# Giving GpSimd the fourth token tile of each batch when the expert results are mixed

## The chip, the cores and the metric

The kernel runs on one core of one Trainium2 chip. The metric is the device time of one execution in microseconds (us). Five engines share the work: TensorE (PE, matrix products into PSUM), VectorE (DVE), ScalarE (ACT), GpSimd (POOL) and SyncE (SP), which here only issues DMAs. They run side by side and meet at semaphores.

## The reference

The program is two transformer layers over 8 batches of 512 tokens with 128 features, in float32. Each layer is attention and then a mixture of experts, with a residual sum around both. The expert part of layer 0 picks 2 of 16 experts for each token, that of layer 1 picks 2 of 8:

```python
x = x + _L0_attn_ref(_layernorm(x), ...)
x = x + _L0_ffn_ref(_layernorm(x), ...)     # 16 experts, top 2
x = x + _L1_attn_ref(_layernorm(x), ...)
x = x + _L1_ffn_ref(_layernorm(x), ...)     # 8 experts, top 2
...
# layer 1's mixture, the same in its last step as layer 0's
topk_values, topk_indices = jax.lax.top_k(router_logits, TOP_K)
topk_weights = jax.nn.softmax(topk_values, axis=-1)
...
mixed_output = jnp.sum(topk_expert_outputs * topk_weights[..., None], axis=2)
```

What matters here is the last step of each mixture: for every token, two result rows of 128 numbers, each times the token's weight for that expert, added to the token's row of `x`.

## The kernel before

`X` holds all 4096 tokens in SBUF as 32 tiles of 128 tokens (128 partitions) by 128 features. A batch is `T` = 4 tiles, and there are `B` = 8 batches. The program is four stages, one after the other, each in a block of its own with a barrier of all engines at its end, after which GpSimd clears the stage's semaphores one by one (line 65): attention of layer 0, `experts` for layer 0 (tag L0), attention of layer 1, `experts` for layer 1 (tag L1).

`experts` routes the tokens, scatters them to DRAM sorted by expert (`x_d`), runs the two matrix products of each expert on tiles of 128 rows, and lets GpSimd scatter every finished tile to its tokens' places in DRAM (`y_d`, indirect DMAs of line 2010). When the last scatter has landed, the stage ends in a mix, and only this mix is touched by the change:

- SyncE's `load(i)` (line 1944) brings the results of batch `i` into one of `MB` = 4 slots of `got`: two DMAs of 256 KB, one for each of the `CH` = 2 chosen experts. The first four batches are loaded at once; the load of batch `i + 4` waits until batch `i` is mixed, since it takes the same slot. All DMAs of the mix are issued from SyncE's queue, in the order of its program.
- VectorE (line 2225) does, for each batch, 4 tiles of the first expert and then 4 tiles of the second, one instruction for a tile, `X = got * gate + X` with both tensors in SBUF. Between the two halves it waits for `mixed1`, since the second half reads what the first has written.
- In the mix of layer 1, SyncE's `write(i)` (line 1949) sends batch `i` of `X` to the output, 256 KB, as soon as it is mixed. In SyncE's queue stand `write(0)`, `load(4)`, `write(1)`, `load(5)` and so on. The mix of layer 0 has no writes.

GpSimd, ScalarE and TensorE have nothing to do in a mix. GpSimd's last work before it is the last scatter.

Of the kernel before, what the change touches and what calls it, by code (L numbers as in the profile page):

```python
# [10 lines left out]
ALU = mybir.AluOpType  # L11
# [5 lines left out]
B, S = 8, 512  # L17
T = S // P
# [55 lines left out]
def build(nc, ins, out, phases="ABCD"):  # L74
    ctx = ExitStack()
    with ctx:
# [29 lines left out]
        if "B" in phases:  # L106
            experts(nc, ins, common, "L0", E0, out)
        if "C" in phases:
            layer1_attention(nc, ins, common)
        if "D" in phases:  # L110
            experts(nc, ins, common, "L1", E1, out)
# [1689 lines left out]
def experts(nc, ins, c, tag, E, out):  # L1801
# [8 lines left out]
    with ExitStack() as ctx:  # L1810
        def sb(name, shape, dt=F32):
            return ctx.enter_context(nc.sbuf_tensor(f"{tag}_{name}", shape, dt))
# [3 lines left out]
        def flag(name):  # L1816

            flags.append(ctx.enter_context(nc.semaphore(f"{tag}_{name}")))
            return flags[-1]

        def after(eng, signal, n):

            if n > 0:
                eng.wait_ge(signal, n)
# [3 lines left out]
        CH = 2  # L1828
# [3 lines left out]
        XB, RB, GB, WB, YB, MB = len(c[f"{tag}_put"]), 2, 6, 4, len(c[f"{tag}_scattered"]), 4  # L1832
        assert NT <= P

        X, ident = c["X"], c["ident"]
# [18 lines left out]
        gate = sb("gate", [P, CH, NG])  # L1854
# [26 lines left out]
        got = sb("got", [P, MB, CH, T, D])  # L1881
# [16 lines left out]
        hidden, acted, y, y_set = flag("hidden"), flag("acted"), flag("y"), flag("y_set")  # L1898
        y_loaded = [flag(f"y_loaded{n}") for n in range(MB)]
        mixed1, mixed2, written = flag("mixed1"), flag("mixed2"), flag("written")  # L1900
        LOADS = 16 * (2 * 4 + 2)
        MADE = 13

# [8 lines left out]
        @block.sync  # L1912
        def _(sp):
            sp.dma_start(wr[:, :], ins[f"{tag}_wr"]).then_inc(wr_loaded, 16)
            if first:
                sp.dma_start(br[:, :], ins["L0_br"].partition_broadcast(P)).then_inc(br_loaded, 16)
            sp.wait_ge(made, 2)
            sp.dma_start(x_d.rearrange("(e r) c -> r e c", e=E)[0:P], empty).then_inc(cleared, 16)
            sp.dma_start(W1[:, :, F + FC:], ins[f"{tag}_b2"].partition_broadcast(P)).then_inc(loads, 16)
            sp.dma_start(W1[:, :, F:F + FC], ins[f"{tag}_b1"]).then_inc(loads, 16)  # L1920
            for n in range(4):
                es = slice(n * E // 4, (n + 1) * E // 4)
                sp.dma_start(W1[:, es, 0:F], ins[f"{tag}_w1"][:, es, :]).then_inc(loads, 16)
                sp.dma_start(W2[:, es, :, :], ins[f"{tag}_w2"][:, es, :, :]).then_inc(loads, 16)

            sp.wait_ge(listing, 1)
            for n in range(XB):
                sp.wait_ge(put[n], 16 * CH * T * len(range(n, B, XB)))
            for n in range(NT):
                at = sp.value_load(slots[0:1, 1, n:n + 1], min_val=0, max_val=E * CAP - P)  # L1930
                if n >= GB:
                    sp.wait_ge(g_turned, n - GB + 1)
                    sp.wait_ge(di_set, n - GB + 1)
                sp.dma_start(xg[:, n % GB, :], x_d[bass.ds(at, P), :]).then_inc(gathered[n % GB], 16)

            for n in range(YB):
                sp.wait_ge(scattered[n], 16 * len(range(n, NT, YB)))
            results = y_d[0:CH * TOK].rearrange("(k n p) d -> p k n d", k=CH, p=P)
            rows = out.rearrange("(n p) d -> p n d", p=P)

            def load(i):
                after(sp, mixed2, T * (i - MB + 1))
                for k in range(CH):
                    sp.dma_start(got[:, i % MB, k, :, :], results[:, k, i * T:(i + 1) * T, :]
                                 ).then_inc(y_loaded[i % MB], 16)

            def write(i):
                sp.wait_ge(mixed2, T * (i + 1))
                sp.dma_start(rows[:, i * T:(i + 1) * T, :], X[:, i * T:(i + 1) * T, :]).then_inc(written, 16)

            for i in range(MB):
                load(i)
            for i in range(B):
                if not first:
                    write(i)
                if i + MB < B:
                    load(i + MB)
            if not first:
                sp.wait_ge(written, 16 * B)

        @block.gpsimd
        def _(pool):
            exact = dict(allow_small_or_imprecise_dtypes=True)
            pool.memset(empty[:, :, 0:D], 0.0).then_inc(made, 1)
            pool.iota(empty[:, :, D:ROW].bitcast(I32), pattern=[[P, E], [0, 1]], base=CH * TOK + NT * P, channel_multiplier=1
                      ).then_inc(made, 1)
            pool.iota(spare[:, :], pattern=[[P, NT]], base=CH * TOK, channel_multiplier=1, **exact).then_inc(made, 1)
            pool.iota(desc[:, :, :], pattern=[[0, T], [-1, E]], base=E, channel_multiplier=0, **exact).then_inc(made, 1)
            pool.iota(dest[:, :, :], pattern=[[P, NG], [TOK, CH]], base=0, channel_multiplier=1).then_inc(made, 1)
            pool.iota(cursor[:, 0, :], pattern=[[CAP, E]], base=0, channel_multiplier=0, **exact).then_inc(made, 1)  # L1970
            pool.iota(column[:, 0:1], pattern=[[0, 1]], base=0, channel_multiplier=1, **exact).then_inc(made, 1)
            pool.iota(column[:, 1:2], pattern=[[0, 1]], base=0, channel_multiplier=P, **exact).then_inc(made, 1)
            pool.memset(tiles[:, :, 0:E], 0.0).then_inc(made, 1)
            pool.memset(ones[:, :], 1.0).then_inc(made, 1)
            pool.memset(ones32[:, :], 1.0).then_inc(made, 1)
            pool.memset(tri[:, :], 1.0).then_inc(made, 1)
            pool.wait_ge(made, 12)

            pool.affine_select(out=tri[:, :], in_=tri[:, :], compare_op=ALU.is_gt, fill=0.0,
                               base=0, pattern=[[1, P]], channel_multiplier=-1).then_inc(made, 1)  # L1980

            def root(i):
                pool.wait_ge(mean, T * (i + 1))
                after(pool, scaled, T * (i - RB + 1))
                pool.tensor_tensor(ve[:, i % RB, :], mv[:, i % RB, :, 1], c["eps"][:, :], ALU.add).then_inc(eps_added, 1)
                pool.wait_ge(eps_added, i + 1)
                pool.tensor_tensor(rstd[:, i % RB, :], ve[:, i % RB, :], c["half"][:, :], ALU.pow).then_inc(rooted, 1)  # L1987

            def put_rows(i):
                if i == 0:  # L1990
                    pool.wait_ge(cleared, 16)
                pool.wait_ge(scaled, T * (i + 1))
                pool.wait_ge(tagged, i + 1)
                pool.wait_ge(placed, i + 1)
                for k in range(CH):
                    for t in range(T):
                        pool.indirect_dma_start(x_d, bass.IndirectOffsetOnAxis(place_i[:, i % XB, k, t:t + 1], 0),  # L1997
                                                XN[:, i % XB, t, k, :], None).then_inc(put[i % XB], 16)

            root(0)  # L2000
            root(1)
            for i in range(B):
                if i + 2 < B:
                    root(i + 2)
                put_rows(i)

            for n in range(NT):
                pool.wait_ge(di_set, n + 1)
                pool.wait_ge(y_set, n + 1)
                pool.indirect_dma_start(y_d, bass.IndirectOffsetOnAxis(di[:, n % YB:n % YB + 1], 0),  # L2010
                                        ys[:, n % YB, :], None).then_inc(scattered[n % YB], 16)

        @block.scalar
        def _(act):
# [29 lines left out]
        def _(dve):  # L2044
# [131 lines left out]
            dve.wait_ge(listing, 2)  # L2176
            dve.wait_ge(loads, LOADS)

# [39 lines left out]
            for i in range(B):  # L2218
                dve.wait_ge(y_loaded[i % MB], 16 * CH * (i // MB + 1))
                for k, mixed in enumerate((mixed1, mixed2)):  # L2220
                    if k:
                        dve.wait_ge(mixed1, T * (i + 1))
                    for t in range(T):
                        n = i * T + t
                        dve.scalar_tensor_tensor(X[:, n, :], got[:, i % MB, k, t, :], gate[:, k, n:n + 1], X[:, n, :],  # L2225
                                                 ALU.mult, ALU.add).then_inc(mixed, 1)
            dve.wait_ge(mixed2, B * T)

        @block.tensor
        def _(pe):  # L2230
# [45 lines left out]
            pe.wait_ge(listing, 2)  # L2276
            pe.wait_ge(loads, LOADS)

# [118 lines left out]
```

## Time and profile before

| | us |
|---|---|
| median of 3 runs | 2020.45 |
| lowest and highest of them | 2016.98, 2028.79 |
| the profiled execution's own time | 2031.6 |
| its span in the trace | 2029.3 |

The time of a run is that of an execution without the profiler; the profile is one further execution. Its span is from the first to the last instruction that the trace shows, and 2.3 us of its own time lie around the span. An instruction's duration is from its start to its end; VectorE starts the next one before the last has ended, so that the distance between starts is shorter than a duration. "Idle before" a group is time in which its engine waited, and the name behind the arrow is what ended the wait. The two mixes lie near 956 to 980 us and near 2000 to 2026 us of the span.

### The profile page before, as it was taken

To read this page: it belongs to the slowest core of one execution; us is meant where nothing else is said; L and a number is where in the kernel's file an instruction comes from. 1 tells how busy PE (TensorE), PEld (TensorE's weight loads), DVE (VectorE), ACT (ScalarE), POOL (GpSimd) and SP (SyncE) were. 2 spreads that over 40 slices of the span, in tenths; PEclk is the share of its full clock that TensorE was granted. 3 is DMA by queue.
4 is the path that set the end of the run, shared out by engine and by line. 5 is a ranking of instruction groups with operands and counts; after the bars stand their busy time and mean duration, and the time that the engine had idled before them with its cause. 6 is when DMAs were issued, how large, how long until landed. Compare 5 with 4: busy or idle time off the path is not lost. (4 is left out here: it accounts for less than half of the span.)

```text
span 2029.3 us, 39821 instructions
## 1 busy us (share of the span) xinstructions
PE 1520.3 (75%) x11726; PEld 979.1 (48%) x11726; DVE 1270.2 (63%) x3477; ACT 892.7 (44%) x1807; POOL 681.3 (34%) x773
## 2 busy tenths in 40 slices
PE   2699999999997423998136898788888979333993
PEld 0223333333333222998024566566665656323993
DVE  2578777777773364554415686877767867353555
ACT  0166666665665001654222555545544434102652
POOL 2202221121100374555153334333433310374552
PEclk9999999999999555999557999999999989756997
DMA  3211111111100531222242434444344441411225
GB/s 93 55 52 52 52 37 40 50 35 51 52 25 1 125 136 45 73 72 79 75 121 88 114 109 127 120 131 121 107 125 116 125 113 47 115 48 50 72 70 148
DMA packets 121565, 165.68 MB, mean 82 GB/s; under 512 B 21458, under 2 KB 94962, under 8 KB 120786
## 3 DMA queue, kind: packets, MB, share of 16 engines
q1 hardware_dynamic: 112530, 145.69, 25.1%
q0 software_dynamic: 8896, 18.30, 2.7%
q8 instruction: 67, 1.10, 0.2%
q14 instruction: 72, 0.59, 0.1%
HBM read 116.04 MB, written 47.60 MB: 81 GB/s over the span
## 5 line engine op out<-in xcount | busy, mean ns | idle before, releaser
L648 DVE TENSOR_REDUCE a_M<-a_F 128x1 f32<-128x512 f32 x512 | 325.7, 682 | 73.7 <-PE a_F L790 72.3
L557 ACT ACTIVATE a_PT<-a_ST 128x512 f32<-128x512 f32 x512 | 276.8, 594 | 137.0 <-PE a_ST L830 134.8
L1392 ACT ACTIVATE c_PT<-c_ST 128x1024 f32<-128x1024 f32 x160 | 163.4, 1021 | 205.7 <-PE c_ST L1702 157.3
L2040 ACT ACTIVATE L_hT<-L_P,L_W1s 128x128 f32<-128x128 f32 x600 | 171.9, 369 | 147.8 <-issue 91.1
L2010 POOL DMA_INDIRECT L_yd<-L_ys,L_di x150 | 163.2, 1088 | 151.6 <-issue 101.9
L830 PE MATMUL a_ST<-a_QS,a_KS 74*128 74x512 bf16 x512 | 173.6, 396 | 21.6 <-ACT a_PT L557 10.0
L790 PE MATMUL a_F<-a_KS,a_QS 72*128 72x512 bf16 x512 | 166.1, 402 | 8.8 <-DVE a_M L648 8.5
L1701 PE MATMUL c_ST<-ident,c_SD 128*128 128x128 f32 x512 | 146.9, 287 | 26.9 <-issue 17.3
L2289 PE MATMUL L_P<-L_xT,L_W1s 128*128 128x128 f32 x1200 | 161.8, 279 | 0.4 <-issue 0.4
L2298 PE MATMUL L_P<-L_W,L_hT 128*128 x1200 | 160.3, 277 | 0.1
L2289 PEld LDWEIGHTS L_P<-L_xT,L_W1s 128*128 128x128 f32 x1200 | 149.5, 196 | 0.7 <-issue 0.7
L2298 PEld LDWEIGHTS L_P<-L_W,L_hT 128*128 128x128 f32 x1200 | 147.3, 193 | 0.6 <-issue 0.4
L809 PE MATMUL a_PV<-a_PT,a_V 128*32 128x512 f32 x1024 | 142.1, 629 | 1.0 <-ACT a_PT L557 1.0
L1997 POOL DMA_INDIRECT L_xd<-L_XN,L_place_i x128 | 124.4, 972 | 53.2 <-issue 37.1
L830 PEld LDWEIGHTS a_ST<-a_QS,a_KS 74*128 74x128 bf16 x512 | 44.0, 98 | 175.0 <-ACT a_PT L557 120.8
L2183 DVE TENSOR_SCALAR L_W1s<-L_W 128x644 f32 x150 | 74.5, 497 | 80.7 <-issue 68.8
L1500 DVE TENSOR_TENSOR c_inc<-c_INC,c_table 128x512 f32<-128x512 f32 x128 | 87.6, 685 | 59.2 <-PE c_INC L1669 58.7
L1702 PE MATMUL c_ST<-c_less,c_pick 128*128 128x128 bf16 x512 | 114.8, 224 | 0.0
L1708 PE MATMUL c_ST<-c_QS,c_KS 126*128 126x384 bf16 (+2 forms) x384 | 108.3, 282 | 0.0
L1707 PE MATMUL c_ST<-c_less,c_pick 128*128 128x384 bf16 (+2 forms) x384 | 107.7, 281 | 0.0
L1513 DVE TENSOR_TENSOR c_SD<-c_DIAG,c_inc 128x512 f32<-128x512 f32 x128 | 87.3, 682 | 25.9 <-PE c_ST L1708 25.9
L1675 PE MATMUL c_DIAG<-c_KS,c_QS 72*128 72x128 bf16 x512 | 76.8, 227 | 34.1 <-DVE c_SD L1513 34.1
(282 smaller groups left out, 3107.2 us busy)
## 6 DMA issues: line engine op xcount, KB each, us to landing
c_QS<-c_q SPq DMA_DIRECT2D x32, 504.0 KB
c_QS<-c_rd SPq DMA_DIRECT2D x32, 378.0 KB
L_xg<-L_xd SPq DMA_DIRECT2D x150, 64.5 KB
a_QS<-a_q SPq DMA_DIRECT2D x32, 288.0 KB
a_KS<-a_k SPq DMA_DIRECT2D x96, 96.0 KB
c_KS<-c_k SPq DMA_DIRECT2D x96, 96.0 KB
L_W<-in_L_w SPq DMA_DIRECT2D x8, 1024.0 KB
L_got<-L_yd SPq DMA_DIRECT2D x32, 256.0 KB, 4.6
```

Source lines behind the costliest of these rows:

```text
L557: act.activation(PT[:, j, kk, :], ST[:, kk, :], ACT.Exp).then_inc(sem(exped), 1)
L648: dve.tensor_reduce(M[:, t, h:h + 1], FB[n % BANKS][:, :], AX_X, ALU.max).then_inc(sem(maxed), 1)
L790: pe.matmul(FB[n % BANKS][:, :], QS[0:STACK, h, t * P:(t + 1) * P], KS[0:STACK, h, :], start=True, stop=True).then_inc(sem(filled), 1)
L809: last = pe.matmul(PV[32 * j:32 * j + 32, :], V[:, kt, QUAD * g + j, :], PT[:, QUAD * (kt // 2) + j, kt % 2, :], start=(kt == 0), stop=(kt ...
L830: pe.matmul(ST[:, kk, :], KS[0:KR0, h, kt * P:(kt + 1) * P], QS[0:KR0, h, :], start=True, stop=True).then_inc(sem(scored), 1)
L1392: act.activation(PT[:, j, :, :], ST[:, :, :], ACT.Exp).then_inc(sem(exped), 1)
L1701: pe.matmul(out, SD[:, g % 2, j, t, :], ident[:, :], start=True, stop=False, is_transpose=True)
L1997: pool.indirect_dma_start(x_d, bass.IndirectOffsetOnAxis(place_i[:, i % XB, k, t:t + 1], 0), XN[:, i % XB, t, k, :], None).then_inc(put[i ...
L2010: pool.indirect_dma_start(y_d, bass.IndirectOffsetOnAxis(di[:, n % YB:n % YB + 1], 0), ys[:, n % YB, :], None).then_inc(scattered[n % YB], 16)
L2040: act.activation(hT[:, n % 2, f, :], PS[2 + 2 * (n % 2) + f // 2][:, (f % 2) * P:(f % 2 + 1) * P], func, bias=W1s[:, n % WB, F + f:F + f + ...
L2289: last = pe.matmul(PS[2 + 2 * (n % 2) + f // 2][:, (f % 2) * P:(f % 2 + 1) * P], W1s[:, n % WB, f * P:(f + 1) * P], xT[:, n % 3, :], start ...
L2298: last = pe.matmul(PS[6 + n % 2][:, 0:D], hT[:, n % 2, f, :], W2[:, bass.ds(e, 1), f, :].rearrange("p a d -> p (a d)"), start=(f == 0), st ...
```

## The change

Of the four tiles of a batch VectorE now mixes three (`OWN` = 3), with the same instructions. GpSimd takes the fourth, and as it is written here it needs two instructions for each expert where VectorE needs one: it multiplies the result tile by the weight in place (`weighed`), and adds it to `X` (`added_up`). The second add waits for the first, and both wait for their product. `load` and `write` now wait for both engines.

```diff
+        weighed, added_up = flag("weighed"), flag("added_up")
+        OWN = T - 1
...
             def load(i):
-                after(sp, mixed2, T * (i - MB + 1))
+                after(sp, mixed2, OWN * (i - MB + 1))
+                after(sp, added_up, CH * (i - MB + 1))
...
             def write(i):
-                sp.wait_ge(mixed2, T * (i + 1))
+                sp.wait_ge(mixed2, OWN * (i + 1))
+                sp.wait_ge(added_up, CH * (i + 1))
...
+            for i in range(B):
+                n = i * T + OWN
+                pool.wait_ge(y_loaded[i % MB], 16 * CH * (i // MB + 1))
+                for k in range(CH):
+                    pool.tensor_scalar(got[:, i % MB, k, OWN, :], got[:, i % MB, k, OWN, :], gate[:, k, n:n + 1], None,
+                                       ALU.mult).then_inc(weighed, 1)
+                for k in range(CH):
+                    pool.wait_ge(weighed, CH * i + k + 1)
+                    after(pool, added_up, CH * i + k)
+                    pool.tensor_tensor(X[:, n, :], X[:, n, :], got[:, i % MB, k, OWN, :], ALU.add).then_inc(added_up, 1)
+            pool.wait_ge(added_up, CH * B)
...
                     if k:
-                        dve.wait_ge(mixed1, T * (i + 1))
-                    for t in range(T):
+                        dve.wait_ge(mixed1, OWN * (i + 1))
+                    for t in range(OWN):
...
-            dve.wait_ge(mixed2, B * T)
+            dve.wait_ge(mixed2, B * OWN)
```

VectorE's instructions at the start of layer 0's mix, before:

```order
L2225 SCALAR_TENSOR_TENSOR X<-L_got,L_gate,X 128x128 [waits L0_y_loaded0]
L2225 SCALAR_TENSOR_TENSOR X<-L_got,L_gate,X 128x128 x3
L2225 SCALAR_TENSOR_TENSOR X<-L_got,L_gate,X 128x128 [waits L0_mixed1]
L2225 SCALAR_TENSOR_TENSOR X<-L_got,L_gate,X 128x128 x3
L2225 SCALAR_TENSOR_TENSOR X<-L_got,L_gate,X 128x128 [waits L0_y_loaded1]
```

The same place now:

```order
L2241 SCALAR_TENSOR_TENSOR X<-L_got,L_gate,X 128x128 [waits L0_y_loaded0]
L2241 SCALAR_TENSOR_TENSOR X<-L_got,L_gate,X 128x128 x2
L2241 SCALAR_TENSOR_TENSOR X<-L_got,L_gate,X 128x128 [waits L0_mixed1]
L2241 SCALAR_TENSOR_TENSOR X<-L_got,L_gate,X 128x128 x2
L2241 SCALAR_TENSOR_TENSOR X<-L_got,L_gate,X 128x128 [waits L0_y_loaded1]
```

Each batch has lost two of its eight instructions there, and the waits stand where they stood. GpSimd's instructions at the end of layer 0's expert stage, which before went from the 79 scatters straight to the block's end, are now:

```order
L2014 DMA L_yd<-L_ys,L_di 20352x128 [waits L0_y_set,L0_di_set] x79
L2021 TENSOR_SCALAR L_got<-L_got,L_gate 128x128 [waits L0_y_loaded0]
L2021 TENSOR_SCALAR L_got<-L_got,L_gate 128x128
L2026 TENSOR_TENSOR X<-X,L_got 128x128 [waits L0_weighed]
L2026 TENSOR_TENSOR X<-X,L_got 128x128 [waits L0_added_up,L0_weighed]
L2021 TENSOR_SCALAR L_got<-L_got,L_gate 128x128 [waits L0_y_loaded1]
```

So 32 instructions have been added to GpSimd in each mix, four for a batch, behind its last scatter.

## Rows read from the trace of the kernel before

**Rows 1.** The page's head: the span, and the whole run's busy time of each engine

```profile
span 2029.3 us, 39821 instructions
...
PE 1520.3 (75%) x11726; PEld 979.1 (48%) x11726; DVE 1270.2 (63%) x3477; ACT 892.7 (44%) x1807; POOL 681.3 (34%) x773
```

**Rows 2.** The groups of instructions in layer 0's mix (956.7:984), then in layer 1's (2000:2030)

```profile
L2225 DVE SCALAR_TENSOR_TENSOR X<-L_got,L_gate,X 128x128 f32<-128x128 f32 x64 | 17.7, 348 | 7.7 <-DMA L_got<-L_yd 7.4
...
L2225 DVE SCALAR_TENSOR_TENSOR X<-L_got,L_gate,X 128x128 f32<-128x128 f32 x64 | 17.7, 347 | 7.4 <-DMA L_got<-L_yd 7.1
```

**Rows 3.** The chain that ended last, from 2000 us: start, length, what

```profile
2002.95 4.71 DMA L_got<-L_yd
...
2008.86 2.20 DVE X L2225 x8
...
2011.08 2.20 DVE X L2225 x8
...
2022.21 1.14 DVE X L2225 x4
```

**Rows 4.** The timeline of SyncE's queue, layer 1's mix

```profile
2007.50 0.38 SPq L1949 DMA_DIRECT2D out_x<-X  x1
...
2007.92 1.34 SPq L1944 DMA_DIRECT2D L_got<-L_yd  x2
```

**Rows 5.** DMA issues from 2000 us: KB each, median us to landing

```profile
L_got<-L_yd SPq DMA_DIRECT2D x16, 256.0 KB, 4.5
```

**Rows 6.** One stretch of layer 1's mix: busy times, granted PE clock, DMA share, GB/s

```profile
2005.00:2019.50 14.50, 0.00 (x0) 0.00 (x0) 13.92 (x51) 0.00 (x0) 0.00 (x0) 0.50 1.12 321
```

**Rows 7.** GpSimd's groups by shape, whole run

```profile
L431 POOL TENSOR_TENSOR a_rot<-a_rot,a_part 128x512 f32<-128x512 f32 x16 | 18.5, 1158 | 35.2 <-ACT a_part L514 35.2
...
L1250 POOL TENSOR_TENSOR c_power<-c_power,c_length 128x128 f32<-128x128 f32 x24 | 10.9, 456 | 1.9
...
L1250 POOL TENSOR_TENSOR c_power<-c_guess 128x128 f32<-128x128 f32 x24 | 9.6, 401 | 55.6 <-DVE c_guess L1457 54.4
...
L1205 POOL TENSOR_SCALAR_AFFINE_SELECT c_table<-c_table 128x2048 f32<-128x2048 f32 x1 | 2.0, 2007 | 7.3 <-ACT c_table L1290 7.3
...
L129 POOL TENSOR_SCALAR_AFFINE_SELECT ident<-ident 128x128 f32<-128x128 f32 x1 | 0.3, 287 | 0.2 <-issue 0.2
```

**Rows 8.** GpSimd's timeline where each instruction waits for the one before

```profile
1038.48 0.46 POOL L1250 TENSOR_TENSOR c_power<-c_power,c_length 128x128 f32<-128x128 f32 x1
1039.01 0.45 POOL L1250 TENSOR_TENSOR c_power<-c_power,c_three_halves 128x128 f32<-128x128 f32 x1
```

**Rows 9.** VectorE's groups by shape, 1040:1050

```profile
L1477 DVE TENSOR_TENSOR c_LP<-c_line,c_DQ 128x384 f32<-128x384 f32 x1 | 0.6, 550 | 0.0
...
L1474 DVE TENSOR_TENSOR c_LP<-c_line,c_DQ 128x96 f32<-128x96 f32 x1 | 0.3, 251 | 0.0
```

**Rows 10.** Timelines near 1215 and 1236 us; last, L1521's min/median/max ns

```profile
1215.23 1.15 POOL L1263 TENSOR_TENSOR c_part<-c_rem,c_part 96x512 bf16<-96x512 f32 x1 [1.50 <-ACT c_part L1342]
...
1216.20 0.21 DVE L1521 TENSOR_TENSOR c_MD<-c_MD,c_M 128x12 f32<-128x12 f32 x1
...
1236.23 0.17 DVE L1521 TENSOR_TENSOR c_MD<-c_MD,c_M 128x12 f32<-128x12 f32 x1
...
L1521 DVE TENSOR_TENSOR c_MD<-c_MD,c_M x32: 160/170/216, 1095.5 to 1720.3; 128x12 f32<-128x12 f32 x32
```

**Rows 11.** Near 654 us: GpSimd's timeline, then VectorE's L169, min/median/max ns

```profile
653.94 1.26 POOL L447 TENSOR_TENSOR a_XC<-a_XA,a_b 128x512 f32<-128x512 f32 x1
...
L169 DVE TENSOR_SCALAR a_ZN<-a_XA,a_tmv,a_trstd x4: 335/336/1207, 654.1 to 655.7; 128x128 f32<-128x128 f32 x4
```

**Rows 12.** Timeline near 722 us, GpSimd and VectorE

```profile
722.69 1.04 POOL L1987 TENSOR_TENSOR L_rstd<-L_ve,half 128x4 f32<-128x4 f32 x1
722.79 0.23 DVE L2079 TENSOR_TENSOR L_eq<-L_work,L_gate 128x64 f32<-128x64 f32 x1
723.05 0.23 DVE L2080 TENSOR_TENSOR L_eq<-L_eq,L_desc 128x64 f32<-128x64 f32 x1
```

**Rows 13.** The clears of semaphores, whole run, min/median/max ns

```profile
L65 POOLq EVENT_SEMAPHORE_RANGE_CLEAR  x219: 37/38/47, 678.1 to 2028.9; - x110
```

## The prediction

> **What bounds the kernel now.** I began with the page's head, to have the span of the profiled execution (2029.3 us) and to see that over the whole run GpSimd is a third busy [rows 1]. That average says nothing of a mix, so I went to the groups of each mix by itself. In both, VectorE runs 64 instructions, 17.7 us busy, and waits 7.7 and 7.4 us, nearly all of it for the first loads [rows 2]. Nothing else computes there. The chain of waits shows what counts: from the last load's landing on, it consists of VectorE alone, eight instructions after eight, to the last one at 2022.21 + 1.14 = 2023.35 us [rows 3]. A batch of eight takes 2011.08 - 2008.86 = 2.22 us, 0.278 us for each, and a mix 8 x 2.22 = 17.8 us [rows 3]. So both mixes lie on the path in full, and what shortens a batch's mix there shortens the kernel. The two mixes are 35.6 us of 2029.3, 1.8%: the whole lever of this change.
>
> The engine that paces the mix is not alone near its limit. The 16 DMA engines are shown full in layer 1's mix, at 321 GB/s [rows 6]. And the slots make a ring: batch 0 was done at 2007.50, when SyncE issued its write; the two loads that reuse its slot were issued from 2007.92 to 2009.26, and a load takes 4.5 us from issue to landing [rows 4, 5]. The second was issued at about 2008.5 and so landed near 2013.0, 5.5 us after batch 0 was done. VectorE came to batch 4 some 3 x 2.22 = 6.7 us after batch 0, so this turnaround is hidden, with 1.2 us to spare.
>
> **The change, part by part.**
>
> VectorE loses 16 instructions in each mix. Alone, a batch would cost it 6 x 0.278 = 1.67 us, 0.55 less, or 16 x 0.278 = 4.4 us in a mix and 8.9 us in both. That is the most that can be had, 0.44%.
>
> GpSimd gains four instructions for each batch. An add of 128x128 with two inputs takes 0.456 us there [rows 7], and where the next waits for it the distance is 1039.01 - 1038.48 = 0.53 us [rows 8]. The product with a column of weights has no row in this trace. From below it is bounded by the one-input select of the same shape, 0.287 us, from above by the product of a tile with itself, 0.401 us [rows 7]. It has one tensor to read but a column to fetch as well, so I take the middle, 0.344 us. The chain is product, product, add, add: 2 x 0.344 + 0.53 + 0.456 = 1.68 us (1.56 to 1.79 by the bounds; 1.9 if each of the four gaps costs the 0.08 us that rows 8 show). So GpSimd by itself needs what VectorE needs by itself: neither hides behind the other with room.
>
> The ring then becomes the limit. A slot goes through one mix and one turnaround in four batches: (1.68 + 5.5) / 4 = 1.80 us. In layer 1's mix, eight loads and four writes, 20 x 0.262 MB = 5.24 MB, must pass before the last batch can start, 16.3 us at 321 GB/s [rows 5, 6]. Counted from 2002, a little before the load with which the chain begins [rows 3], batch 7 ends at 2018.3 + 1.7 = 2020.0, 3.3 us before the present 2023.35. With the first batches' loads no faster than before, I count about 3 us in each mix, 6 in both, if the two engines don't disturb each other.
>
> But they do read the same memory, and two places in the trace show VectorE held by GpSimd. VectorE's 128x12 maximum with both inputs in SBUF takes 0.17 us by itself and 0.21 us where it starts inside a GpSimd instruction that reads SBUF; it then ends at 1216.41, 0.03 us behind that one's end at 1216.38 [rows 10]. Its 32 instructions have a median of 0.170 and a longest of 0.216 [rows 10]; I count five near the latter, all of them inside a GpSimd add. And a VectorE tensor_scalar of 0.336 us took 1.207 where it started at 654.1, behind a GpSimd add that ran from 653.94 to 655.20, and it ended within 0.1 us of that one's end [rows 11]. Against a hold for the whole instruction stands the power on 128x4, 1.04 us long: two VectorE instructions with two SBUF inputs ran inside it in their usual 0.23 us [rows 12]. It reads four columns and computes long. So what excludes the other engine seems to be the reading, not the instruction.
>
> I size the reading by slopes. GpSimd's adds: (1158 - 456) / 384 = 1.83 ns for a column, 0.234 us for 128 columns; its one-input select: (2007 - 287) / 1920 = 0.90 ns, 0.115 us; for the product 0.115 to 0.21 (the last by 0.401 x 0.234 / 0.456) [rows 7]. VectorE with two inputs: (550 - 251) / 288 = 1.04 ns, 0.133 us [rows 9]. Between two readings of VectorE, 0.278 - 0.133 = 0.145 us are free. An add then pushes VectorE back by 0.234 - 0.145 = 0.09 us, a product by 0 to 0.07: the batch costs VectorE 1.67 + 2 x 0.09 + 2 x 0.04 = 1.93 us. GpSimd in turn waits up to one VectorE reading each time: 1.68 + 4 x 0.13 = 2.2 us. The slower of them counts, 2.2 us against 2.22 now, or about 2.15 if not every wait is the longest. That is 0.07 x 16 = 1.1 us gained in both mixes.
>
> The Trainium skill, "SBUF — State Buffer", section "Who interferes with whom", states it more sharply: a VectorE instruction with two SBUF inputs contends with a GpSimd instruction that reads SBUF, and whichever is second blocks fully until the first has finished. The trace agrees that there is a block, and its 0.23 us inside the power's 1.04 speak against a hold for the whole duration; what the rule would make of the sum is the second rival below.
>
> The small rest: two more semaphores mean two more clears in each expert stage. One takes 0.038 us [rows 13]; even at twice that, four are 0.3 us. SyncE's extra waits come where it waits anyway. What was queued behind those waits, the loads and the write, now leaves with the slower of two engines. At the end of the kernel that is the last write. In sum: -1.1 + 0.3, about -1 us.
>
> The profiled execution took 2031.6 us, of which its span is 2029.3; it lies 11 us above the median of 2020.45, and I put the difference of -1 us on the median: 2019.5.
>
> **The rivals.**
>
> *No hold at all.* If the cases of rows 10 and 11 don't carry over, both engines run at 1.7 and the ring and the DMA set the pace: -6 + 0.3, 2014.7 us, and at the very most -8.9, 2011.6. For it: the hold in rows 10 costs only 0.04 us. Against it: it is so each time, five out of five.
>
> *Whole instructions take turns.* If one engine's instruction excludes the other's from start to end, a batch costs 6 x 0.278 + 2 x 0.456 + 2 x 0.344 = 3.27 us; the mixes grow by 16 x 1.05 = 16.8 us, 2037.5 us. It ends on the other side. It decides from a batch of 2.22 + 10.1 / 16 = 2.85 us on. For it speaks rows 11, where the wait was nearly a whole instruction; against it rows 12. It is also what the Trainium skill's page "SBUF — State Buffer" says of such a pair.
>
> *GpSimd is starved.* VectorE's next instruction has started before the last has ended (0.347 us long, 0.278 apart [rows 2, 3]), so GpSimd may find no gap until VectorE waits. Then VectorE does batches 0 to 3 in 4 x 1.67 = 6.7 us, GpSimd its first batch only until 8.4, and the load into its slot lands at 13.9. The others land every 1.68, the last at 18.9, and both engines in turn need 2 x 1.68 for it: 22.3 us against 17.8: +4.5 in each mix, 2029.8 us. The reading gaps above speak against it.
>
> *The change does nothing at all* can't be: the mixes are on the path and VectorE's share falls.
>
> **How the numbers follow.** The forecast, a change between -4 and +3 us, gets 0.6; no hold 0.15; starvation 0.13; turns by whole instructions 0.12. A measurement of this kernel tells about 0.5%, 10.1 us, from no change. No case gains that much, so faster has 0.04, for the scatter of the runs, whose own spread was 2016.98 to 2028.79. Slower needs whole turns, or starvation with a bad draw: 0.14. The rest, 0.82, is no change. The range reaches from the largest possible gain to starvation and a little over it, 2011.5 to 2033.
>
> **What would show it.** VectorE's 48 instructions in each mix: if held, some of them last longer than 0.35 us and start over 0.278 apart; if not, a batch of six takes 1.67. GpSimd's adds: 0.456 us if free, up to 0.6 if they wait for a reading, 0.7 and more with whole turns. GpSimd's products at 0.29 to 0.40. VectorE's waits for loads should reappear after batch 3 if the ring binds. The last instruction before the last write should be GpSimd's. I am wrong if the distance from batch to batch is under 1.95 or over 2.5 us; most likely then by the price of the product, which no row gives, or by how a hold is handed on.

## The result: about 17 us slower, and the profile after

| | before | after |
|---|---|---|
| runs | 4 | 4 |
| median, us | 2018.72 | 2039.56 |
| lowest and highest, us | 2016.87, 2028.79 | 2033.11, 2045.46 |
| ratio | | 1.0086 [1.0056, 1.0117] |

The ratio means 17.4 us more, 11 to 24 by its interval; the two medians of four runs lie 20.8 us apart. The forecast was 2019.5 us, the upper end of its range 2033.0.

The page's head shows no other work that has grown: GpSimd is 36 us busier and VectorE about as busy as before [rows 1], though it runs 32 instructions less.

```profile
span 2031.4 us, 39905 instructions
...
PE 1510.5 (74%) x11726; PEld 973.0 (48%) x11726; DVE 1268.8 (62%) x3445; ACT 891.8 (44%) x1807; POOL 717.0 (35%) x837
```

Its span is only 2.1 us longer than that of before. The two profiled executions differ ahead of the mixes too: here layer 0's mix began 6.6 us earlier (955.2 against 961.8). So I don't compare spans, but what each mix and the end of its stage take. The groups of layer 0's mix (955:984), then of layer 1's (2000:2030):

```profile
L2241 DVE SCALAR_TENSOR_TENSOR X<-L_got,L_gate,X 128x128 f32<-128x128 f32 x48 | 17.3, 422 | 8.4 <-DMA L_got<-L_yd 8.1
L2021 POOL TENSOR_SCALAR L_got<-L_got,L_gate 128x128 f32<-128x128 f32 x16 | 10.7, 675 | 5.7 <-DMA L_got<-L_yd 5.7
L2026 POOL TENSOR_TENSOR X<-X,L_got 128x128 f32<-128x128 f32 x16 | 7.9, 494 | 1.1
...
L2241 DVE SCALAR_TENSOR_TENSOR X<-L_got,L_gate,X 128x128 f32<-128x128 f32 x48 | 17.1, 417 | 8.3 <-DMA L_got<-L_yd 8.0
L2021 POOL TENSOR_SCALAR L_got<-L_got,L_gate 128x128 f32<-128x128 f32 x16 | 10.7, 676 | 5.5 <-DMA L_got<-L_yd 5.5
L2026 POOL TENSOR_TENSOR X<-X,L_got 128x128 f32<-128x128 f32 x16 | 8.1, 507 | 1.1
```

VectorE's 48 instructions take about as long as the 64 did [rows 2]: 0.42 us each instead of 0.347. A product takes GpSimd 0.675 us, twice what I had reckoned with. The timeline of layer 0's mix shows the pace:

```profile
958.41 1.39 POOL L2021 TENSOR_SCALAR L_got<-L_got,L_gate 128x128 f32<-128x128 f32 x2 [0.62 <-DMA L_got<-L_yd]
...
961.01 1.32 POOL L2021 TENSOR_SCALAR L_got<-L_got,L_gate 128x128 f32<-128x128 f32 x2
...
963.51 1.46 POOL L2021 TENSOR_SCALAR L_got<-L_got,L_gate 128x128 f32<-128x128 f32 x2
...
966.03 1.28 POOL L2021 TENSOR_SCALAR L_got<-L_got,L_gate 128x128 f32<-128x128 f32 x2
...
968.36 1.28 POOL L2021 TENSOR_SCALAR L_got<-L_got,L_gate 128x128 f32<-128x128 f32 x2
...
970.69 1.28 POOL L2021 TENSOR_SCALAR L_got<-L_got,L_gate 128x128 f32<-128x128 f32 x2
```

From one pair of products to the next it is 970.69 - 968.36 = 2.33 us in the later batches, where VectorE alone had needed 2.22 [rows 3], and 2.60, 2.50 and 2.52 us in batches 1 to 3, which make the larger part of the mix's loss. From the first instruction of a mix to its last, layer 0's takes 20.07 us (18.44 before) and layer 1's 19.96 (18.2): 3.4 us more in both. That is a fifth of the loss. It is GpSimd that ends each mix, 1.5 us behind VectorE.

The rest stands behind the mix. At the end of a stage each engine's queue has a DRAIN before it meets the others at the barrier; run 7 will show that GpSimd's waits for scatters that are still landing. The instructions of the block's end, first before, then after (min/median/max ns, first and last start):

```profile
L1810 POOLq DRAIN  x2: 8442/8770/9098, 955.4 to 1998.8; - x2
L1810 SPq DRAIN  x2: 7/64/122, 972.3 to 2025.9; - x2
...
L1810 DVEq DRAIN  x2: 10/10/10, 980.5 to 2023.6; - x2
```

```profile
L1810 SPq DRAIN  x2: 13/70/127, 967.1 to 2023.0; - x2
...
L1810 DVEq DRAIN  x2: 10/10/10, 974.1 to 2019.3; - x2
...
L1810 POOLq DRAIN  x2: 7169/7497/7825, 975.5 to 2020.7; - x2
```

VectorE's drain takes 0.01 us. GpSimd's takes 7 to 9, and it did so before as well: it began at 955.4, just ahead of the last scatter's own start, and was over at 964.5, while VectorE mixed until 980.2. Nobody waited for it. Now GpSimd mixes first, and its drain begins when its mix is done: 975.5 + 7.8 = 983.3 in layer 0, 2020.7 + 7.2 = 2027.9 in layer 1. VectorE had been done at 974.1, and SyncE, with the last write landed, at 2023.0. So 7.8 us lie bare in layer 0, where nothing else was still under way, and 4.9 in layer 1, 12.7 in both. The next stage shows it: its first VectorE instruction waited 4.20 us before, and now 13.86.

```profile
987.69 1.76 DVE L1409 MEMSET c_V<- 128x2048 f32 x1 [13.86 <-PEq L61]
```

12.7 + 3.4 makes 16.1 us of the measured 17.4. The runs below test both parts. Runs 4, 5, 9 and 10 are single executions. The kernel before spreads over 20 us and more from chip to chip and run to run, so these four tell by their traces, hardly by their times.

### The profile page after: what moved, and what is told of

The parts are those of the page before. It is cut to its first block and busy times, and to the rows that moved or that the text cites. A ratio compares the mean times of both kernels' runs of the same rounds, so it can differ in the third digit from the quotient of the medians.

```text
span 2031.4 us, 39905 instructions
## 1 busy us (share of the span) xinstructions
PE 1510.5 (74%) x11726; PEld 973.0 (48%) x11726; DVE 1268.8 (62%) x3445; ACT 891.8 (44%) x1807; POOL 717.0 (35%) x837
```

## The experiments

**1. The wait alone.** The kernel before, with GpSimd made to stay in its program until the mix is over; it does no work there.

```diff
                                         ys[:, n % YB, :], None).then_inc(scattered[n % YB], 16)
+            pool.wait_ge(mixed2, B * T)
```

> The kernel before, with one thing added: after its last scatter GpSimd waits until VectorE has finished the whole mix (no work is moved to it). Theory D (the loss is GpSimd's drain at the end of the expert stage, 7.8 us and 7.2 us long, which before ran beside the mix and now begins only after it): the drain is exposed in full behind layer 0's mix, +7.8 us, and behind layer 1's as far as the last write does not cover it, 7.2 - 2.3 = 4.9 us; in all about +12.7 us, with both drains 7 to 8 us long in the trace. Theory C (the two engines hold each other up in the mix, and that is the loss): no change, since nothing overlaps.

Measured: 2034.06 us (12 runs) against 2020.82 (29 runs), ratio 1.0057 [1.0037, 1.0076], so 11.5 us, 7.5 to 15, where I had expected 12.7. The mixing instructions are as before, the drain comes late:

```profile
L2226 DVE SCALAR_TENSOR_TENSOR X<-L_got,L_gate,X x128: 343/347/352, 957.1 to 2022.0; 128x128 f32<-128x128 f32 x128
...
L1810 SPq DRAIN  x2: 7/64/122, 968.3 to 2024.8; - x2
L1810 POOLq DRAIN  x2: 7169/7493/7817, 976.4 to 2022.5; - x2
```

With nothing moved, about two thirds of the loss are there. The late drain alone makes it.

**2. Help in the first half only.** GpSimd takes the fourth tile of batches 0 to 3, VectorE mixes batches 4 to 7 whole. GpSimd's drain can then begin in mid-mix.

```diff
+        HELPED = 4
...
-            for i in range(B):
+            for i in range(HELPED):
                 n = i * T + OWN
...
-                    for t in range(OWN):
+                    for t in range(own(i)):
```

> The changed kernel, but GpSimd takes the fourth tile only in batches 0 to 3 of each mix, VectorE takes all four in batches 4 to 7. Theory D: GpSimd is done some 9 us before VectorE, its drain of 7 to 8 us lies beside VectorE's last four batches, and what is left is the slower pace of four batches, 4 x 0.1 to 0.2 us in each mix: +1 to +2 us over the kernel before, 14 to 15 under the changed kernel. Theory C: half of the loss stays, +8 us over before.

Measured: 2018.91 us (12 runs), ratio to before 0.9994 [0.9976, 1.0013]. GpSimd's drain now ends with or ahead of the others, at 961.8 + 7.8 = 969.6 and 1997.3 + 7.2 = 2004.5:

```profile
L1810 POOLq DRAIN  x2: 7169/7497/7825, 961.8 to 1997.3; - x2
...
L1810 DVEq DRAIN  x2: 10/10/10, 969.4 to 2005.0; - x2
```

The loss is gone. The help in four batches brings nothing that the times could show: the two mixes last 18.05 and 18.22 us, 18.44 and 18.19 before.

**3. Drain first, then mix.** The changed kernel with a drain between GpSimd's last scatter and its first product.

```diff
 
+            pool.drain()
             for i in range(B):
```

> The changed kernel with one more drain of GpSimd between its last scatter and its first product. If the drain's length is a debt that the scatters leave (theory D, first form): the extra drain takes 7 to 8 us and the one at the stage's end falls under 1 us; the extra one ends about 3 us after the first load has landed, so each mix starts some 3 us late for GpSimd, and the kernel comes to -13 + 6 = -7 us against the changed kernel, +9 over before. If every drain of GpSimd costs 7 to 8 us once indirect DMAs have run (second form): the drain at the end stays 7 to 8 us and the kernel gets 6 us slower than the changed kernel. Theory C: no gain, at least +3.

Measured: 2026.66 us (10 runs), ratio to before 1.0032 [1.0011, 1.0053], 6.5 us. The added drain, and the one at the block's end:

```profile
L2017 POOLq DRAIN  x2: 8442/8772/9101, 944.4 to 1989.4; - x2
...
L1810 POOLq DRAIN  x2: 45/46/46, 973.6 to 2017.1; - x2
```

A drain is paid once: the second one has nothing left and takes 0.05 us, though 32 instructions lie between. So GpSimd's mix is not what is drained; the scatters are. What remains is a slower mix in which GpSimd starts late: in layer 0 VectorE began at 951.01, GpSimd only at 953.68, when the added drain was over. From the first instruction of a mix to its last it is 22.4 us (18.44 before) and 21.3 (18.2), 7.0 us more in both, against the 6.5 measured.

**4. VectorE alone.** Nobody mixes the fourth tile.

```diff
-                after(sp, added_up, CH * (i - MB + 1))
...
-                sp.wait_ge(added_up, CH * (i + 1))
...
-            for i in range(B):
-                n = i * T + OWN
-                pool.wait_ge(y_loaded[i % MB], 16 * CH * (i // MB + 1))
...
-            pool.wait_ge(added_up, CH * B)
```

> The changed kernel without GpSimd's share: nobody mixes the fourth tile of a batch, so that part of the sum is missing from the result. It shows VectorE's three tiles by themselves. Expected: 1.65 to 1.7 us for a batch as long as its load is there, then the ring of four slots and its 5.5 us, 1.8 us for a batch; each mix 14 to 15.5 us instead of 17.8. Its difference to the pace in the changed kernel (2.33 us a batch) is what GpSimd's share costs there. GpSimd's drain again beside the mix, so that the kernel is 5 to 7 us faster than before by either theory.

Measured: a single run, 2018.26 us. VectorE's timeline in layer 0's mix, then the first and the last piece of layer 1's:

```profile
953.76 1.79 DVE L2228 SCALAR_TENSOR_TENSOR X<-L_got,L_gate,X 128x128 f32<-128x128 f32 x6 [6.98 <-DMA L_got<-L_yd]
956.36 7.20 DVE L2228 SCALAR_TENSOR_TENSOR X<-L_got,L_gate,X 128x128 f32<-128x128 f32 x24 [0.81 <-DMA L_got<-L_yd]
963.82 1.79 DVE L2228 SCALAR_TENSOR_TENSOR X<-L_got,L_gate,X 128x128 f32<-128x128 f32 x6 [0.25 <-DMA L_got<-L_yd]
966.32 3.49 DVE L2228 SCALAR_TENSOR_TENSOR X<-L_got,L_gate,X 128x128 f32<-128x128 f32 x12 [0.71 <-DMA L_got<-L_yd]
...
1992.37 1.79 DVE L2228 SCALAR_TENSOR_TENSOR X<-L_got,L_gate,X 128x128 f32<-128x128 f32 x6 [6.81 <-DMA L_got<-L_yd]
...
2008.06 1.79 DVE L2228 SCALAR_TENSOR_TENSOR X<-L_got,L_gate,X 128x128 f32<-128x128 f32 x6 [0.44 <-DMA L_got<-L_yd]
```

Twenty-four instructions, batches 1 to 4, take 7.20 us, 1.80 a batch, where one that waits for no load takes 1.71, and longer waits for loads come back behind them. Layer 0's mix lasts 16.05 us, 2.4 less than before. Layer 1's, which also writes, lasts 2008.06 + 1.79 - 1992.37 = 17.5 us, only 0.7 less than before: there VectorE waits for loads in all but one of its batches. So with GpSimd's tile free the two mixes gain 3.1 us, not the 6 of the prediction. What it had too fast are the loads: layer 1's last batch could start 2008.06 - 1988.75 = 19.3 us after the first load was issued. The prediction's time for that, 2018.3, lies 16.9 us behind the first load's issue in the trace of before, at 2001.42.

**5. GpSimd alone.** Only the fourth tile is mixed.

```diff
-                after(sp, mixed2, OWN * (i - MB + 1))
...
-                sp.wait_ge(mixed2, OWN * (i + 1))
...
-            for i in range(B):
-                dve.wait_ge(y_loaded[i % MB], 16 * CH * (i // MB + 1))
...
-            dve.wait_ge(mixed2, B * OWN)
```

> The changed kernel without VectorE's share: only the fourth tile of each batch is mixed, by GpSimd, the other three are missing from the sum. It gives GpSimd's prices with nothing beside them. If the 0.64 us of its product in the changed kernel come from being held by VectorE, the product takes 0.3 to 0.4 us here, as the prediction had it; if the product with a column is that dear by itself, 0.6 us or more. The adds should take 0.45 us. The drains at the stage ends stay 7.8 and 7.2 us long.

Measured: a single run, 2036.96 us, against 2028.48 (17 runs) on that chip. GpSimd's groups and timeline in layer 0's mix:

```profile
L2019 POOL TENSOR_SCALAR L_got<-L_got,L_gate 128x128 f32<-128x128 f32 x16 | 9.5, 605 | 6.7 <-DMA L_got<-L_yd 6.7
L2024 POOL TENSOR_TENSOR X<-X,L_got 128x128 f32<-128x128 f32 x16 | 7.3, 453 | 1.1
...
963.20 1.19 POOL L2019 TENSOR_SCALAR L_got<-L_got,L_gate 128x128 f32<-128x128 f32 x2
...
965.38 1.19 POOL L2019 TENSOR_SCALAR L_got<-L_got,L_gate 128x128 f32<-128x128 f32 x2
```

Undisturbed, a product takes 0.605 us, and a batch 965.38 - 963.20 = 2.18 us. GpSimd by itself is as slow with one tile as VectorE was with four.

**6. A drain between the routing scatters and the results' scatters.** GpSimd issues 64 scatters in each stage for the routing, and 79 and 71 for the results.

```diff
                 put_rows(i)
+            pool.drain()
```

> The changed kernel with one more drain of GpSimd between the 64 scatters of the routing and those of the experts' results, where GpSimd has nothing to do. If the drain's length grows with the number of indirect DMAs since the last drain (theory D, debt): the 143 and 135 of a stage leave 7.8 and 7.2 us, about 0.055 us each, so the drains at the stage ends fall to about 4.3 and 3.9 us, and the kernel to 7 us under the changed kernel. If the length is bounded by something that the last few scatters leave, or is the same for any number: 7.8 and 7.2 us as before, no gain.

Measured: 2041.68 us (4 runs), ratio to before 1.0064 [1.0046, 1.0082]; the changed kernel itself had 1.0086 [1.0056, 1.0117] against its own runs of before. The two intervals overlap, so the times don't decide; the drains do. The added drain begins while 8 scatters of the routing are still ahead of it on GpSimd in layer 0, and 10 in layer 1. It, the last routing scatter of layer 0, and the drain at the end:

```profile
L2010 POOLq DRAIN  x2: 15361/16615/17869, 780.5 to 1844.3; - x2
...
789.61 0.96 POOL L2001 DMA_INDIRECT L_xd<-L_XN,L_place_i  x1 [0.30 <-issue]
...
L1810 POOLq DRAIN  x2: 5852/6179/6506, 981.9 to 2029.2; - x2
```

At the end 6.506 us remain for 79 scatters and 5.852 for 71: 0.0824 us for each, in both layers. A routing scatter has the same price: the added drain is over at 780.5 + 15.4 = 795.9, 5.31 us after the last of the 64 has ended at 790.57, and 5.30 after it in layer 1, 0.083 for each. Yet without the added drain the one at the end takes 7.825 and 7.169, only 1.32 more than with it, what 16 scatters cost and not 64. So the length grows with the number of scatters, but most of the routing's share is gone by the end of the stage without any drain. The added one pays 5.3 us and saves 1.3.

**7. A drain behind every scatter of results**, and behind each batch's eight scatters of the routing.

```diff
                 put_rows(i)
+                pool.drain()
...
                                         ys[:, n % YB, :], None).then_inc(scattered[n % YB], 16)
+                pool.drain()
```

> The changed kernel with a drain of GpSimd behind each batch's 8 routing scatters and behind each of the 150 scatters of results, where GpSimd waits for the next tile some 0.8 us anyway. Debt: each drain takes about 0.05 to 0.1 us (0.4 to 0.7 for eight), hides in that wait, and the drains at the stage ends fall under 1 us: 12 us under the changed kernel, +3 over the kernel before. If every drain behind a scatter has a price of its own of 1 us or more, the experts' stage becomes slower than GpSimd's 1.9 us per tile allows, and the kernel gets slower than the changed one by up to 150 x 1 us.

Measured: 2265.94 us (6 runs), ratio to before 1.1184 [1.1158, 1.1211]. The drains behind the results' scatters, and those of the end:

```profile
L2017 POOLq DRAIN  x150: 2213/2534/4453, 816.7 to 2228.4; - x150
...
L1810 POOLq DRAIN  x2: 53/53/53, 1107.5 to 2254.4; - x2
```

My expectation was wrong: a drain behind one scatter is not 0.08 us but 2.5. It begins some 0.2 us ahead of the scatter's start; the scatter lands 2.2 us (median) after its start, and the drain ends 0.07 behind that. So it waits for the landing. In the kernel before, the early drain takes 9.098 us in layer 0 and 8.442 in layer 1, and the late one 7.825 and 7.169, 1.27 more in both. Two lines of before, layer 0, tell what these 1.27 are:

```profile
955.68 0.96 POOL L2010 DMA_INDIRECT L_yd<-L_ys,L_di  x1 [0.30 <-issue]
958.09 14.18 SPq L1944 DMA_DIRECT2D L_got<-L_yd  x16
```

The early drain starts at 955.38 and the last scatter ends at 956.65, 1.27 us later; from there the drain takes the 7.83 of the late one. The landing adds nothing: the first load, which waits for it, was issued at 958.09, while the drain ran until 964.48. So behind many scatters the 0.08 for each decide, and the landing runs beside them; behind one the landing decides. The debt can't be paid in small change.

**8. ScalarE weighs.** In batches 0 to 3 ScalarE, idle in the mix, does the product of the fourth tile, GpSimd only the add; batches 4 to 7 are VectorE's.

```diff
+            for i in range(HELPED):
+                n = i * T + OWN
+                act.wait_ge(y_loaded[i % MB], 16 * CH * (i // MB + 1))
+                for k in range(CH):
+                    act.activation(got[:, i % MB, k, OWN, :], got[:, i % MB, k, OWN, :], ACT.Copy,
+                                   scale=gate[:, k, n:n + 1]).then_inc(weighed, 1)
```

> A candidate for a faster kernel: in batches 0 to 3 ScalarE, idle in the mix, multiplies the fourth tile's two results by their weights in place, GpSimd only adds them to X, VectorE has three tiles; in batches 4 to 7 VectorE has all four, so that GpSimd's drain is hidden. GpSimd's chain is then two adds, about 1.0 us a batch, and VectorE's three tiles should pace the first four batches at 1.8 to 1.9 us instead of 2.22: 1.3 to 1.7 us gained in each mix, 3 us in all, 0.15% under the kernel before. If the adds alone hold VectorE up as much as adds and products together, no gain.

Measured: 2028.88 us (12 runs) against 2028.48, ratio 0.9998 [0.9988, 1.0007]. The groups of layer 1's mix (1999:2022):

```profile
L2252 DVE SCALAR_TENSOR_TENSOR X<-L_got,L_gate,X 128x128 f32<-128x128 f32 x51 | 15.8, 378 | 7.5 <-DMA L_got<-L_yd 7.3
L2030 POOL TENSOR_TENSOR X<-X,L_got 128x128 f32<-128x128 f32 x8 | 3.8, 472 | 9.3 <-ACT L_got L2067 8.7
L2067 ACT ACTIVATE L_got<-L_got,L_gate 128x128 f32<-128x128 f32 x8 | 2.8, 393 | 12.7 <-DMA L_got<-L_yd 12.7
```

The product takes 0.393 us on ScalarE, which was idle. GpSimd's drains are hidden again (over at 977.5 and 2021.0, when VectorE still mixed), and still nothing is gained that the times could show: VectorE's mean is 0.378 us instead of 0.347, so it is held beside the adds. The two mixes last 17.77 and 17.92 us, 0.9 us less than before together, where I had expected 3.

**9 and 10. What holds VectorE.** GpSimd adds the fourth tile unweighed in all batches (9), or in place of each add only clears the result tile, which writes to SBUF and reads nothing there (10).

```diff
                 for k in range(CH):
-                    pool.tensor_scalar(got[:, i % MB, k, OWN, :], got[:, i % MB, k, OWN, :], gate[:, k, n:n + 1], None,
-                                       ALU.mult).then_inc(weighed, 1)
-                for k in range(CH):
-                    pool.wait_ge(weighed, CH * i + k + 1)
                     after(pool, added_up, CH * i + k)
...
-                    pool.tensor_tensor(X[:, n, :], X[:, n, :], got[:, i % MB, k, OWN, :], ALU.add).then_inc(added_up, 1)
+                    pool.memset(got[:, i % MB, k, OWN, :], 0.0).then_inc(added_up, 1)
```

(The upper part is in both, the last pair of lines in 10 alone.)

> The changed kernel without GpSimd's products: it adds the fourth tile's results unweighed, so that tile's sum is not the reference's. VectorE's three tiles as in the changed kernel. In the run where ScalarE weighs, an add beside VectorE's pair of instructions cost VectorE 0.2 us (VectorE's instruction 0.55 us long instead of 0.35). If an add holds VectorE by its reading alone as predicted (0.09 us), a batch takes 1.69 + 0.18 = 1.87 us; if by 0.2 us, 2.1 us; if by its whole 0.456 us, 2.6 us. The drains stay 7.8 and 7.2 us long and exposed.

> The same, with each of GpSimd's adds replaced by a fill with zeros of the tile of got that nobody reads any more: a GpSimd instruction of the same shape that reads nothing. The fourth tile is not mixed at all. If only GpSimd's reading holds VectorE, VectorE's 48 instructions all take 0.34 to 0.35 us and a batch 1.61 to 1.7 us until the ring binds at 1.8; if any GpSimd instruction that touches SBUF does, some of them take 0.45 us and more.

Measured: a single run each, 2027.83 and 2034.35 us, beside a single 2011.79 of before on that chip; the late drain is in both. VectorE's and GpSimd's instructions in both mixes, run 9 (with two single ones from its timeline), then run 10:

```profile
L2237 DVE SCALAR_TENSOR_TENSOR X<-L_got,L_gate,X x96: 337/347/645, 959.3 to 2015.6; 128x128 f32<-128x128 f32 x96
L2022 POOL TENSOR_TENSOR X<-X,L_got x32: 452/453/640, 959.3 to 2013.9; 128x128 f32<-128x128 f32 x32
...
961.90 0.64 DVE L2237 SCALAR_TENSOR_TENSOR X<-L_got,L_gate,X 128x128 f32<-128x128 f32 x1 [0.35 <-DMA L_got<-L_yd]
961.95 0.45 POOL L2022 TENSOR_TENSOR X<-X,L_got 128x128 f32<-128x128 f32 x1 [1.46 <-DMA L_got<-L_yd]
```

```profile
L2237 DVE SCALAR_TENSOR_TENSOR X<-L_got,L_gate,X x96: 343/347/353, 959.3 to 2021.8; 128x128 f32<-128x128 f32 x96
L2022 POOL MEMSET L_got<- x32: 205/205/206, 959.4 to 2020.7; 128x128 f32 x32
```

Beside GpSimd's clears VectorE is never longer than 0.353 us; beside its adds it is up to 0.645. The pair at 961.90 shows how: GpSimd's add ends at 962.40, VectorE's instruction 0.15 us behind it, though it started 0.04 us ahead of the add. In all 32 of run 9's VectorE instructions over 0.4 us it is 0.147 to 0.150. That is near one reading of 128 columns by my slope of 0.133 (that step of the prediction, [rows 9]), as if VectorE read only when GpSimd was through; the trace doesn't show the reading itself. A clear is only 0.205 us long; by the same 0.15 behind its end a held instruction would take 0.36 to 0.38 us, and none is that long. Run 9's batches in layer 0 come 2.47, 2.43, 2.04, 2.21, 2.16 and 2.17 us apart from batch 1 on, between my cases; run 10's 1.79, 1.82, 1.78, 1.72, 1.76 and 1.71. The difference between adds and clears is what the Trainium skill, "SBUF — State Buffer", section "Who interferes with whom", says: a VectorE instruction with two SBUF inputs contends with a GpSimd instruction that reads SBUF, not with one that only writes it. Here the trace agrees with both halves.

## Why the prediction was wrong

**The step that failed is one that isn't there: what GpSimd still had to do at the end of the stage.** The part on the change costs GpSimd's four instructions, VectorE's, SyncE's waits and the clears, and the only word on what comes after the mix is "at the end of the kernel that is the last write". I had taken GpSimd as idle in a mix. It wasn't: its queue ran a DRAIN of 9.1 and 8.4 us there, in the trace of before, off the chain and so in no view that I had asked for. The change put a mix of 20 us ahead of it. What remains bare is what the others don't cover, 7.8 and 4.9 us. Run 1 makes that loss without the work (11.5 us), run 2 does work without that loss (-0.06%), run 3 shows that the drain belongs to the scatters. That is 12.7 of 17.4 us, and no rival of mine had it: the rival of turns by whole instructions gave 2037.5 us, close to the result, by a cause that accounts for 3.4 us, not for the 16.8 which it claimed. Its nearness is luck.

**GpSimd's product: the term was mis-sized.** I took 0.344 us, the middle of 0.287 and 0.401; run 5 measured 0.605 with nothing beside it, outside both bounds. The rows I bounded it by were a select and the product of a tile with itself; neither fetches a number for each partition. Whether that is what makes it dearer, no run shows. GpSimd's chain for a batch is 2.18 us, not 1.68 (or 1.9 with gaps). Against the 2.22 of before, that alone leaves 0.04 us a batch, 0.6 in all, before any hold.

**The hold: right in kind, too small for the add.** I had it last only for the reading, 0.09 us for an add and 0.04 for a product, and thought that an instruction as a whole excludes nothing. Single instructions of the changed kernel, beside a product and beside an add:

```profile
968.36 0.64 POOL L2021 TENSOR_SCALAR L_got<-L_got,L_gate 128x128 f32<-128x128 f32 x1
968.45 0.45 DVE L2241 SCALAR_TENSOR_TENSOR X<-L_got,L_gate,X 128x128 f32<-128x128 f32 x1
...
970.26 0.45 POOL L2026 TENSOR_TENSOR X<-X,L_got 128x128 f32<-128x128 f32 x1
970.30 0.56 DVE L2241 SCALAR_TENSOR_TENSOR X<-L_got,L_gate,X 128x128 f32<-128x128 f32 x1
```

In the steady batch after the change VectorE's six starts are 0.48, 0.38, 0.26, 0.38, 0.26 and 0.57 us apart. Unheld, as in run 10, they would be 0.26 each, and 0.38 where the second half waits for the first. So the two adds push it by 0.22 and 0.19, and the two products by 0.11 each: 1.70 + 0.41 + 0.22 = 2.33 us, which is the pace. Beside an add VectorE ends 0.15 us behind the add's end, as in run 9. Beside a product it isn't held so long: it is 0.45 us long and ends at 968.90, while the product runs to 969.00. So a wait for the end of GpSimd's instruction fits the adds and not the products. Even an add costs far less than its 0.45 us, as I read it since the wait overlaps with the start of VectorE's own instruction and with its own spacing of 0.26. The rival of whole turns was right about the block by an add and wrong about its price: it added up durations, 3.27 us for a batch, where 2.33 was measured. Rows 12, which I held against it, stand: VectorE ran unheld beside a power on 128x4. No run here tried an instruction of that kind.

**GpSimd's waits for VectorE.** I gave it up to 0.13 us for each of four, 0.52 at most. In the steady batches measured are 0.035 to 0.05 for a product (0.640 and 0.655 against 0.605), 0.05 for the first add, none for the second, 0.14 in all: 2.18 + 0.14 = 2.32. In batches 1 to 3 they are 2.50 to 2.60 less 2.18, 0.32 to 0.42. I predicted 1.93 for VectorE and 2.2 for GpSimd. Measured is 2.33 for both at the end of the mix; before that VectorE runs ahead at 2.02 to 2.09 us a batch.

**The loads, mis-sized too.** The prediction had a batch of 1.80 us from the ring of slots and 3 us gained in each mix without a hold; run 4 gained 2.4 and 0.7. Its 1.80 us in layer 0 are no proof of the ring's: batches 1 to 3 use slots for the first time. From batch 4 on, where slots are used again, the batches start 2.04, 2.50 and 1.71 us apart in layer 0 and 2.56, 2.35 and 2.23 in layer 1. In the changed kernel this limit no longer decides. In the first 14.5 us of layer 1's mix, which cover the same stage of it as rows 6 do, the DMA engines are a little less busy, 1.06 and 303 GB/s where it was 1.12 and 321 [rows 6]:

```profile
2000.53:2015.03 14.50, 0.00 (x0) 0.00 (x0) 13.60 (x39) 0.00 (x0) 13.41 (x23) 0.50 1.06 303
```

**What held.** The clears are 4 more at 0.038 us, 0.15 in all. That the most to be had was under 0.5% was right too; it was 3.1 us, 0.15%. My range was too low because only rivals of the mix itself were in it.

**A better version.** None was found. Runs 2 and 8, which hide the drain, are equal to before within about 0.2%: the hold takes back nearly all that VectorE's smaller share gives, and in layer 1 the loads leave only 0.7 us to be had at all.

## What to carry to other kernels

Before you give an idle engine work at the end of a stage, read its queue to the barrier, not its compute rows: what it does there unseen (here GpSimd's drain after its indirect DMAs) moves behind the new work, and it costs what the other engines no longer cover. Such help, if any, belongs where the drain still fits behind the others' work. And price an operation by a row with the same kinds of operands: GpSimd's product with a column of scalars took 1.5 to 2.1 times what the rows of its size suggested. Measure the upper bound of the gain stage by stage as well: one mix here could give 2.4 us and its twin, which also writes, 0.7.

## What the runs showed of the hardware

- GpSimd's DRAIN after indirect DMAs takes 0.082 to 0.083 us for each scatter of 128 rows, counted from the last one's end on GpSimd (64 of the routing 5.31 us, 79 of the results 6.506, 71 of them 5.852, run 6), and it doesn't end before the last has landed (2.2 us after its start, run 7). A second drain takes 0.05 us (runs 3 and 7). 143 and 135 scatters, 64 of them of the routing, made 7.825 and 7.169 us, what 95 and 87 would. What the drain does in that time, and where the price of the other 48 went, stays open.
- GpSimd's tensor_scalar with a column of multipliers, 128x128 float32, takes 0.605 us; its add with two full inputs 0.453; the same product on ScalarE 0.393.
- A VectorE instruction with two SBUF inputs beside a GpSimd add with two ends 0.15 us behind the add, up to 0.645 us long in place of 0.35 (run 9). Beside GpSimd's product with a column it takes 0.45 us and ends 0.1 us before the product does. Beside a GpSimd clear it keeps its time (run 10).
